# First attention stage: score products over the 32 stack rows of one key group instead of all 128, without masked key stacks

## The reference, cut to what matters

```
NUM_HEADS = 16; NUM_KV = 4; HEAD_DIM = 8; SCALE = HEAD_DIM ** 0.5
q = (x @ Wq + bq)   # 16 heads of 8, in 4 groups of 4
k = (x @ Wk + bk)   # 4 key heads of 8, one to a group
v = (x @ Wv + bv)
scores = jnp.einsum('bghnd,bhsd->bghns', q, k)
attn = softmax(scores / SCALE)
out = jnp.einsum('bghns,bhsd->bghnd', attn, v)
return out @ Wo + bo
```

## Time and profile before

| what | value |
|---|---|
| time, median of 3 runs | 1564.23 us (1564.1 to 1566.51) |
| the profiled execution's own time | 1565.83 us |
| its span, first to last instruction | 1563.8 us |
| PE matmuls busy | 1427.5 us, 91% |
| PE weight loads busy | 1145.8 us, 73% |
| DVE busy | 1106.1 us, 71% |
| ACT busy | 957.5 us, 61% |
| POOL busy | 582.1 us, 37% |
| mean granted TensorE clock | 0.949 of 2.4 GHz |
| first attention, from its first transposes to its last addition | about 302 to 669 us of the span |

### The profile page before, as it was taken

One profiled execution on the slowest core, in us unless ns is written; L12 is line 12 of the kernel. 1 busy time (PEld: TensorE's weight loads), 2 busy tenths in 40 slices (PEclk: granted clock), 3 DMA queues, 4 the chain that ended last, 5 costly groups with the idle time before them and its releaser, 6 DMA issues.

```text
span 1563.8 us, 26546 instructions
## 1 busy us (share of the span) xinstructions
PE 1427.5 (91%) x9270; PEld 1145.8 (73%) x9270; DVE 1106.1 (71%) x2377; ACT 957.5 (61%) x1710; POOL 582.1 (37%) x551
## 2 busy tenths in 40 slices
PE   5699999789999999969999997999968999989998
PEld 5588888555555555457888886799956777768998
DVE  3766766768888888556676676477758888876765
ACT  5455555436666666646555556577736666668886
POOL 4466666500000000004666665377720111126664
PEclk9999999859999999959999996799979999999999
DMA  6000000000000000000000004000000000000000
GB/s 171 0 1 1 1 1 1 0 0 1 1 1 1 1 1 1 1 0 1 1 1 1 1 1 164 1 2 1 2 0 1 2 1 2 2 1 1 15 14 28
DMA packets 13314, 16.79 MB, mean 11 GB/s; under 512 B 768, under 2 KB 10496, under 8 KB 12928
## 3 DMA queue, kind: packets, MB, share of 16 engines
q1 hardware_dynamic: 13184, 15.11, 3.2%
HBM read 13.01 MB, written 2.10 MB: 10 GB/s over the span
## 4 chain that ended last, share of the span: by engine, by line
PE 81%; DVE 8%; ACT 7%; issue 3%; DMA 1%; POOL 0%; SPq 0%; DVEq 0%; POOLq 0%; ACTq 0%
PE PS L593 19%; PE PS L621 10%; PE PS L1721 9%; PE PS L1734 8%; PE PS L750 3%; PE PS L729 3%; PE PS L737 3%; ACT AR L842 2%; PE PS L707 2%; PE PS L1095 2%; PE PS L1070 2%; PE PS L1099 2%; PE PS L417 2%; PE PS L1052 1%; PE PS L1080 1%
## 5 line engine op out<-in xcount | busy, mean ns | idle before, releaser
L530 POOL TENSOR_TENSOR RR<-AR,RR 128x512 fp32r<-128x512 f32 x150 | 193.9, 1293 | 531.7 <-ACT RR L553 531.6
L567 ACT ACTIVATE AR<-PS 128x512 f32<-128x512 f32 x224 | 134.1, 598 | 195.6 <-PE PS L593 194.3
L509 DVE TENSOR_TENSOR AR<-AR,PS 128x512 f32<-128x512 f32 x224 | 153.8, 687 | 132.3 <-PE PS L593 131.1
L911 DVE TENSOR_REDUCE AR<-PS 128x2 f32<-128x512 f32 x256 | 173.6, 687 | 54.3 <-PE PS L729 53.6
L842 ACT ACTIVATE AR<-PS 128x512 f32<-128x512 f32 x256 | 149.7, 600 | 101.3 <-PE PS L737 100.0
L593 PE MATMUL PS<-XHI,WG 128*128 128x512 f32 x448 | 175.8, 392 | 0.0
L593 PE MATMUL PS<-XHI,WU 128*128 128x512 f32 x448 | 174.4, 389 | 0.0
L513 DVE TENSOR_TENSOR AR<-AR,PS 128x512 f32<-128x512 f32 x224 | 154.0, 687 | 8.0 <-POOL RR L530 0.3
L1721 PE MATMUL PS<-XHI,SL 128*128 128x256 f32 x576 | 133.5, 287 | 2.3 <-DVE XTR L1886 1.9
L729 PE MATMUL PS<-XLO,XHI 128*128 128x512 f32 x256 | 127.6, 505 | 8.6 <-DVE AR L911 6.0
L1721 PE MATMUL PS<-XLO,SL 128*128 128x256 f32 x576 | 133.0, 286 | 1.5 <-DVE XTR L1886 1.3
(11 more groups left out here) (297 smaller groups left out, 3371.7 us busy)
## 6 DMA issues: line engine op xcount, KB each, us to landing
X<-in_x SPq DMA_DIRECT2D x4, 512.0 KB, 6.4
RAWZ<-in_zone_up SPq DMA_DIRECT2D x8, 256.0 KB, 4.8
RAWZ<-in_zone_down SPq DMA_DIRECT2D x8, 256.0 KB, 5.5
out_x<-X SPq DMA_DIRECT2D x4, 512.0 KB, 3.2
AR<-in_w SPq DMA_DIRECT2D x1, 1792.0 KB, 11.8
XT<-in_w SPq DMA_DIRECT2D x1, 1608.0 KB, 8.7
XT<-in_sel SPq DMA_DIRECT2D x1, 896.0 KB, 8.0
SM<-in_small SPq DMA_DIRECT2D x1, 857.5 KB, 7.0
```

Source lines behind the costliest of these rows:

```text
L509: v.tensor_tensor(PRD[:, m % 2, :], SIL[:, m % 2, :], bank(2 + m % 2), ALU.mult).then_inc(S.prod, 1)
L530: g.tensor_tensor(HL[k % 3], GAT[:, m % 2, :], HH[k % 3].bitcast(F32), ALU.subtract).then_inc(S.h_lo, 1)
L567: act.activation(SIL[:, m % 2, :], bank(m % 2), ACT.Silu).then_inc(S.silu, 1)
L911: v.tensor_reduce(MX[:, 2 * m:2 * m + 2], bank(m % 2).rearrange("p (h k) -> p h k", h=2), AX.X, ALU.max)\
```

## The change

`KS0[b % 3]` becomes the plain key stack, 128 x 256, written by one scalar_tensor_tensor at position 3; `KSF0`, the four tensor_scalar copies, `k_chain` and the part at position 4 go. S and T take only the 32 partitions of one group, by `rows_of(m)`, for stationary and moving operand alike. S becomes two matmuls of 256 columns each, heads 2jp and 2jp+1 of one group, into the two halves of the bank; T stays one matmul of 512 columns. S walks through its 16 products group by group now, as T did before; since S runs four products ahead, S and T of one position take rows of different groups. The second half of the query stack is needed at the second S of a batch, no longer at the fifth. `smax` writes its two maxima with a stride, to where they stood before.

```
--- before.py
+++ after.py
@@ -170,7 +170,7 @@
                 "z_hi z_lo z_lo2 pooled r_pe r_act r_dve idx sel_u sel_d u_pe gelu h_hi h_lo z_pe sum back x_half x_new")
         BOTH = ("stats_done dve_chain m_chain r_chain rstd_in xn tr xt kv qh qs v s_pe smax mm mt qs2 st_pe "
                 "exp av os ot ao aot_pe aot out x_new st_new zero xb")
-        kinds = {"f0": FFN0, "f1": FFN1, "a0": BOTH + " k_chain kx q qx ks",
+        kinds = {"f0": FFN0, "f1": FFN1, "a0": BOTH + " kx q qx ks",
                  "a1": "m_chain r_chain kv qh qs v s_pe smax mm mt qs2 st_pe exp av os ot ao aot_pe aot out x_new zero xb kl kp_pe kp_hi "
                        "kp_lo raw_in blank prep_pe prep_hi prep_lo prep_copy"}
 
@@ -663,11 +663,10 @@
         AO0 = ar(6144, 256)
         AOT0 = ar(6400, 256)
         KX0 = ar(6656, 256)
-        KSF0 = ar(6912, 256)
         QX0 = XN.rearrange("p u t h -> p (u t h)")
         QS0 = [XHI[:, u * 1024:(u + 1) * 1024] for u in range(3)]
         QH0 = XHI[:, 3072:4096]
-        KS0 = [XLO[:, u * 1024:(u + 1) * 1024].rearrange("p (g k) -> p g k", g=4) for u in range(3)]
+        KS0 = [XLO[:, u * SEQ:(u + 1) * SEQ] for u in range(3)]
         KH0 = XLO[:, 3072:3328]
         NS0 = NH0
 
@@ -684,6 +683,10 @@
 
         LEAD = 4
 
+        def rows_of(m):
+
+            return slice(m // 4 * 32, m // 4 * 32 + 32), m // 2 % 2, m % 2
+
         def a0_pe(n):
             S = ST[n]
             pe = nc.tensor
@@ -718,23 +721,26 @@
                 last.then_inc(S.mt, 1)
 
             def scores(b, m):
-                k, j, gp = m // 8, m // 2 % 4, m % 2
+                rows, k, jp = rows_of(m)
                 if m == 0:
                     pe.wait_ge(S.ks, b + 1)
                     if b == 0:
                         pe.wait_ge(S.xt, NC)
-                if m in (0, 4):
-                    pe.wait_ge(S.qs, 2 * b + m // 4 + 1)
+                if m < 2:
+                    pe.wait_ge(S.qs, 2 * b + m + 1)
                 wait(pe, S.smax, NS0 * b + m - 1)
-                pe.matmul(bank(m % 2), QS0[b % 3][:, j * SEQ + k * P:j * SEQ + (k + 1) * P], KS0[b % 3][:, 2 * gp:2 * gp + 2, :],
-                          start=True, stop=True).then_inc(S.s_pe, 1)
+                for i, j in enumerate((2 * jp, 2 * jp + 1)):
+                    last = pe.matmul(bank(m % 2)[:, i * SEQ:(i + 1) * SEQ],
+                                     QS0[b % 3][rows, j * SEQ + k * P:j * SEQ + (k + 1) * P], KS0[b % 3][rows, :],
+                                     start=True, stop=True)
+                last.then_inc(S.s_pe, 1)
 
             def scores_t(b, m):
                 if m < 2:
                     pe.wait_ge(S.qs2, 2 * b + m + 1)
                 wait(pe, S.exp, NS0 * b + m - 1)
-                g, k, jp = m // 4, m // 2 % 2, m % 2
-                pe.matmul(bank(2 + m % 2), KS0[b % 3][:, g, k * P:(k + 1) * P], QS0[b % 3][:, jp * 512:(jp + 1) * 512],
+                rows, k, jp = rows_of(m)
+                pe.matmul(bank(2 + m % 2), KS0[b % 3][rows, k * P:(k + 1) * P], QS0[b % 3][rows, jp * 512:(jp + 1) * 512],
                           start=True, stop=True).then_inc(S.st_pe, 1)
 
             def values(b, g):
@@ -877,7 +883,7 @@
             S = ST[n]
             v = nc.vector
             norm_dve(n)
-            rchain, mchain, kchain = Chain(v, S.r_chain), Chain(v, S.m_chain), Chain(v, S.k_chain)
+            rchain, mchain = Chain(v, S.r_chain), Chain(v, S.m_chain)
 
             def vals(b):
                 v.wait_ge(S.kx, b + 1)
@@ -888,14 +894,9 @@
                                            T.bvb.rearrange("p (g d) -> p g d", g=4), ALU.add)
                 last.then_inc(S.v, 1)
 
-            def key_stacks(b, part):
-                if part == 0:
-                    wait(v, S.st_pe, NS0 * (b - 2))
-                    kchain.link(v.scalar_tensor_tensor(KSF0, KH0.bitcast(F32), T.masks[:, 1:2], KX0, ALU.mult, ALU.add))
-                for g in (2 * part, 2 * part + 1):
-                    last = v.tensor_scalar(KS0[b % 3][:, g, :], KSF0, T.masks[:, 2 + g:3 + g], None, ALU.mult)
-                if part:
-                    last.then_inc(S.ks, 1)
+            def key_stacks(b):
+                wait(v, S.st_pe, NS0 * (b - 2))
+                v.scalar_tensor_tensor(KS0[b % 3], KH0.bitcast(F32), T.masks[:, 1:2], KX0, ALU.mult, ALU.add).then_inc(S.ks, 1)
 
             def stacks(b, half):
                 v.wait_ge(S.qh, 2 * b + half + 1)
@@ -908,8 +909,9 @@
                 if m == 0:
                     wait(v, S.mm, b)
                 v.wait_ge(S.s_pe, NS0 * b + m + 1)
-                v.tensor_reduce(MX[:, 2 * m:2 * m + 2], bank(m % 2).rearrange("p (h k) -> p h k", h=2), AX.X, ALU.max)\
-                    .then_inc(S.smax, 1)
+                g, k, jp = m // 4, m // 2 % 2, m % 2
+                v.tensor_reduce(MX.rearrange("p (k j g) -> p k j g", k=2, j=4)[:, k, 2 * jp:2 * jp + 2, g],
+                                bank(m % 2).rearrange("p (h k) -> p h k", h=2), AX.X, ALU.max).then_inc(S.smax, 1)
 
             def maxima(b):
                 v.wait_ge(S.smax, NS0 * (b + 1))
@@ -956,8 +958,8 @@
                         smax(b, s)
                     if m == 2 and far:
                         vals(i + 2)
-                    if m in (3, 4) and far:
-                        key_stacks(i + 2, m - 3)
+                    if m == 3 and far:
+                        key_stacks(i + 2)
                     if m == 5 and done:
                         normalise(i - 1, 1)
                     if m in (8, 9) and far:
```

## The result

The changed kernel takes 1649.29 us (median of 4 runs, 1647.76 to 1656.61), the kernel before 1564.29 beside it: a ratio of 1.0549, interval 1.0515 to 1.0583. It is 85 us slower. The forecast had the sign and not the size: 13 us.

What follows compares the result with a forecast made beforehand. PE was taken to bound most of a step, then ACT and DVE; 14 full steps at 0.77 us gave 10.8, the edge steps 0.4, 0.6 and 1.0, together 12.8: 1577 us, range 1549 to 1588.

Steps and rivals of the forecast that it cites:

- The rival: Whole stage: fewer busy rows or more waits hold PE at 1.2 GHz, some 10 us a step, +70; chance 0.03.
- Against it: the same mix of work holds 1.00 with PE idle for 1.4 us a step: Argument against a low clock: the kernel before keeps the full clock despite that PE idle time in each step.
- The cost of a change of split: PE switching between 128 and 32 rows: 0.10 us each, 0.15 where the load was hidden; 1.01 a step net.
- near the column rows: Basis for 0.10 and 0.15: trace rows at 2.4 GHz, T to `values` 0.33 us against T to `turn` 0.23.
- the far row: Alternating 128- and 33-row attention matmuls at 1.2 GHz: at least 0.15 us a change, about 0.17 at full clock.
- T beside S: T overlapping the second S matmul: 0.05 us at each of four T (positions 1, 4, 5, 6), 0.20 a step.
- The faster rival: T runs beside S at once and the split is free: 0.5 to 0.6 us a step, 1556 us; chance 0.23.
- The forecast of 0.77 us a step: Full step's net loss: changes of split 1.01, less 0.20 for T and 0.04 for DVE; 10.8 us over 14 steps.
- stretches C and D: From `queries` at position 4 to DVE's second shift; PE decides until 458.53, then ACT, then DVE from position 11.
- stretch D: From S at position 11 to DVE's second shift: 6.46 us, decided by DVE, PE only just in time; expected longer.
- the "same" rival: Neither gain nor split cost, or both cancel: 1563 us, between 1561 and 1567; chance 0.15.
- What would show it: Signs listed beforehand: loader idle, `queries` to S above 0.75 us, T 0.3 behind S, step about 21.2 at clock 1.00.

Runs made afterwards that it cites:

- T's kernel: Kernel before with masked stacks kept, S in the new order as two matmuls over 128 rows, T alone over 32 rows: 1725.4 us, second run 2396.96.

## Why the prediction was right in sign and wrong in size

**The clock: the step that failed.** The rival was written down, "with fewer rows at work or more waits the chip might hold PE at 1.2 GHz", and its price, "over half the steps, +70", is close to the 85 that were measured. That is luck in part: it took 10 us for each step in half of them, while of the first thirteen steps one grew by 10 and most by some 3, and steps 13 to 15 by 27 together. It got 0.03, because of the step "Against it: the same mix of work holds 1.00 with PE idle for 1.4 us a step". That row is of products over 128 rows. It says that idle time of this size leaves the clock alone; of rows it says nothing, and the change replaced all 128-row score products, 32 matmuls a step that take some 0.23 us each, 7.4 of PE's 18.99. With the rows alone changed, 1565.87 becomes 1668.28. With PE at work 39.55 of 40 us the clock is still 0.50. With the waits filled, 128 rows give 1590 and 32 rows 1658. The trace of before has no row for products over 32 rows, so nothing stood against +70 as an upper end; it was left out of the range, whose 1588 is 61 us short. "TensorE: Matmul & The Clock Gate", Part 1, of the Trainium skill describes the gate as set by "how busy the PE has been recently". The 39.55 of 40 us at 0.50 don't agree with busy time as the profile counts it; the measurement decides.

**The cost of a change of split: right in kind, too small.** It was taken at 0.10 where the load was bare and 0.15 where it was hidden; measured were 0.19 between rows at the full clock, 0.23 behind `turn` and 0.28 behind `queries`. The bounds 0 to 0.29 hold all three. The rows that the choice went by, "near the column rows", were at the right clock but of splits by columns (0.10), and the far row, by rows at 1.2 GHz, gave the better estimate, 0.17. That is where the choice went wrong. "TensorEngine Tiling (Array Packing)", Key Properties, of the Trainium skill, which says that a change of the mode drains the array, agrees with the loader's idle 0.24 and 0.33.

**T beside S: right in kind, too small.** The prediction took 0.05 at each of four T, because three loads "stand in a row". They don't: loads of S and T, in different row groups, are 0.01 apart, and T starts 0.01 behind S. The whole 0.21 is gained at each. The faster rival's premise, 0.11 at each, was too small too.

**The sum of both.** The forecast of 0.77 us a step, 10.8 in all, held two wrong sizes of opposite sign. At the full clock stretches C and D together take 13.94 us where they took 13.99, and stretch D, said to grow, is 6.47 from 415.00 to 421.47, as before. Positions 0 to 3 were not seen at the full clock in this kernel, but with the four fillers over 128 rows a whole step is only 0.27 us longer than before. So by its own steps the forecast fails as well: without the clock this would have been at or near the "same" rival, with "losses and gains cancel" as its reason. As an estimate from that 0.27, all but some 4 us of what the full steps lost is the clock's. That the kernel came out slower, as forecast, is luck: it is slower by another mechanism than the one in the sum.

**DVE: right for the full clock.** Busy time is down by 16.6 us in 16 batches, 1.04 each, and the idle time before the reductions is up from 54.3 to 141.8. A step with that work in it takes as long as one without, 23.74 against 23.7, in steps with low clock too.

**What would show it.** Loader idle by "issue" before S and `queries` to S longer than 0.75 came true. T "still 0.3 behind S", the step of 21.2 us and a longer stretch D did not. The last signal, a clock below 1.00, named the right rival.

**Left open.** What the chip counts: the runs show that products over 32 rows lose the clock, and not by what they lose it. Why some steps fall whole and others at their border alone; how much of one product being worse than two is the clock, beyond the 2.80 us a step of T's kernel; the long run of T's kernel; and whether a mix of 128-row and 32-row products exists that holds the clock without extra work.

## What to carry to other kernels

When an edit makes matmuls use fewer rows of the array, ask first what it does to TensorE's granted clock, and give that rival a chance of its own, since a whole stage at the other level outweighs any term of the sum; a clock that held with other products is no evidence. Pair products of different row groups next to each other, and keep them away from full ones: each change cost about 0.2 us here and each pairing gave about as much back. Where a stage starts at 1.2 GHz in its own waits, a few short full-array products in them may pay; here it was 0.33%.

## What the runs showed of the hardware that was not expected

- With score products over 32 rows the clock was granted at 0.50 with PE busy 39.55 of 40 us, and with T's alone 40.00 of 40. With fillers over 32 rows it fell from 1.00 while PE was busy two us out of two.
- A T matmul issued behind two S matmuls started 0.01 us behind the first and 0.21 ahead of the second (407.00, 407.01, 407.22), in another row group.
- Sixteen extra matmuls, 6.8 us of PE time, made the kernel before faster by about 5 us (0.33%, interval 0.17 to 0.5).
- 32-row products lost the clock where 128-row products with 96 rows of zeros in the key stack held it (1668.28 against 1565.87 us).
